# Block products at constant addresses first, then those at register addresses, in the dense passes of a graph network kernel

## What is computed

```python
for l in range(2):
    h = h @ Wt[l].T + bt[l]
    g = tanh(h[row] @ Wg[l] + bg[l])
    norm = g * dinv[row] * dinv[col]
    out = segment_sum(norm[:, None] * h[row], col)
    h = relu(out + h)
```

## Time and profile before

| | |
|---|---|
| time of three runs | 3939.83, 3942.78, 3947.1 us (median 3942.78) |
| the profiled execution | 3943.99 us |
| its span from first to last instruction | 3942.1 us |
| pass 0 (gathers from 607 us) | to 1146 us |
| pass 1 (with the building of items) | 1190 to 1741 us |
| block pass 4 | 3018 to 3456 us |
| block pass 5 | 3487 to 3926 us |

### The profile page before, as it was taken

The page is one execution under the profiler, slowest core; times in us unless marked ns, Lnnn a source line. Parts: engine busy times, 40 slices in busy tenths (PEclk is TensorE's granted clock), DMA queues, the critical chain, the costliest instruction groups (busy, mean ns, idle before and its releaser), DMA issues.

```text
span 3942.1 us, 59800 instructions
## 1 busy us (share of the span) xinstructions
PE 2308.3 (59%) x15144; PEld 2029.6 (51%) x15171; DVE 2210.6 (56%) x5804; ACT 1280.8 (32%) x3481; POOL 2021.6 (51%) x2076
## 2 busy tenths in 40 slices
PE   5972223666655666756756545554556666676665
PEld 4971213555534555545656544454445555665565
DVE  8988916777763555553665565778775222132212
ACT  4210011333220333335777754777762000000000
POOL 2777777777747777735777744777750000000000
PEclk9985555666666665556565667778778999989999
DMA  2210001122131344433333324444441222212221
GB/s 81 68 40 4 4 20 58 53 53 52 53 50 52 117 126 124 130 73 89 81 81 81 80 31 123 129 131 131 131 83 59 75 74 80 74 54 75 79 74 53
DMA packets 151496, 298.20 MB, mean 76 GB/s; under 512 B 49862, under 2 KB 67579, under 8 KB 151091
## 3 DMA queue, kind: packets, MB, share of 16 engines
q0 software_dynamic: 72704, 138.94, 15.1%
q1 hardware_dynamic: 74214, 145.16, 11.7%
q10 hardware_dynamic: 4430, 12.43, 1.0%
HBM read 249.70 MB, written 46.67 MB: 75 GB/s over the span
## 4 chain that ended last, share of the span: by engine, by line
POOL 40%; PE 24%; issue 18%; DVE 11%; ACT 3%; DMA 2%; DVEq 1%; POOLq 0%; ACTq 0%; SPq 0%
POOL arena L710 18%; PE psum L1495 15%; POOL pool L710 13%; POOL rec_dram L687 7%; DVE pool L2118 4%; PE psum L1420 3%; PE psum L1225 2%; ACT pool L882 2%; POOL ACC L710 2%; DVE ACC L2338 1%; PE psum L1263 1%; PE psum L1449 1%; ACT pool L811 1%; PE psum L1100 1%; DVE pool L1717 1%
## 5 line engine op out<-in xcount | busy, mean ns | idle before, releaser
L710 POOL DMA_INDIRECT arena<-tab_dram,tblk x832 | 794.0, 954 | 409.1 <-issue 249.5
L1495 PE MATMUL psum<-arena,pool 128*128 x4096 | 568.7, 293 | 301.3 <-DVE pool L2118 293.8
L1495 PEld LDWEIGHTS psum<-arena,pool 128*128 128x128 f32 x4096 | 527.4, 189 | 343.3 <-issue 342.7
L2118 DVE CAST pool<-pool 128x1024 f32<-128x1024 bf16 x256 | 177.1, 694 | 673.4 <-PE psum L1495 672.8
L687 POOL DMA_INDIRECT rec_dram<-arena,ACC x400 | 395.2, 988 | 196.4 <-issue 119.2
L710 POOL DMA_INDIRECT pool<-tab_dram,arena x416 | 401.1, 964 | 131.4 <-issue 126.4
L1543 PE MATMUL psum<-pool 128*128 128x136 f32 (+1 forms) x1664 | 362.0, 399 | 80.2 <-DVE pool L2262 73.9
L1543 PEld LDWEIGHTS psum<-pool 128*128 128x128 f32 x1664 | 335.3, 290 | 92.4 <-issue 51.7
L1379 PE MATMUL psum<-pool 128*128 128x128 f32 x832 | 192.8, 425 | 294.0 <-DMA pool<-tab_dram,arena 200.4
L710 POOL DMA_INDIRECT pool<-tab_dram,tblk x272 | 277.8, 1021 | 126.3 <-issue 78.6
L1379 PEld LDWEIGHTS psum<-pool 128*128 128x128 f32 x832 | 179.8, 328 | 298.4 <-DVE pool L2131 132.3
(11 more groups left out here) (378 smaller groups left out, 4760.6 us busy)
## 6 DMA issues: line engine op xcount, KB each, us to landing
pool<-items_dram SPq DMA_DIRECT2D x128, 512.0 KB, 3.3
items_dram<-pool SPq DMA_DIRECT2D x128, 256.0 KB, 2.5
pool<-dst_dram SPq DMA_DIRECT2D x104, 256.0 KB, 3.5
arena<-tab_dram,tblk POOLq DMA_INDIRECT x832
HN<-in_edge_attr_dram ACTq DMA_DIRECT2D x23, 500.0 KB
pool<-tab_dram,arena POOLq DMA_INDIRECT x416
rec_dram<-arena,ACC POOLq DMA_INDIRECT x400, 2.1
pool<-tab_dram,tblk POOLq DMA_INDIRECT x272
```

The source lines that it names most:

```text
L710: nc.gpsimd.indirect_dma_start(to[:, j, :], None, tab_dram[k], bass.IndirectOffsetOnAxis(ap=idx[:, G * g + j:G * g + j + 1], axis=0)).then ...
L1495: last = nc.tensor.matmul(psum[:, bass.ds(vals[BITE + j] * P, P)], item, of, start=False, stop=False)
L2118: v.tensor_copy(bite32[slot % 4], bite16[slot]).then_inc(s_cast, 1)
```

## The change

The items are numbered in another way. FIRSTS = 640 items have fixed places: item 25 d + s is, for destination block d and source block s, the **first** tile of d that has edges of s (625 of them and 15 empty ones). The other TILES = 416 items are, one for each tile, **later** items: the source block that begins before the tile's start and still goes on in it. (The edges of a destination block are sorted by source block, so a tile needs at most one later item.) ITEMS is 1056, in 132 packs of 8.

In a block pass the 80 packs of first items come first. Their matmuls have constant addresses and no registers are loaded for them (of packs 78 and 79 only one product each is made, so there are 626). Then come 52 packs of later items, whose 16 block numbers are loaded into registers as before, now from a constant address of `where`. The whole pass is written out; the loop is gone. Items are stored as uint8 instead of bf16, so that a pack has 128 KB. SP loads one pack in a DMA into eight buffers, and DVE casts into six `bite32` buffers instead of four.

The setup has fewer steps on DVE (24 linked small instructions, two rounds of seven over 416 elements, two at the end, against 30, 14 over 512 elements, and six), and one PE round trip less. SP writes six small lists instead of four. In pass 1 DVE makes the ends of the later items (two instructions over 832 elements); ACT and PE make those of the 640 first items only. Packs are built from group 8 on instead of 9, 132 instead of 128, so the last group of pass 1 has three packs instead of two.

```diff
+FIRSTS = 640
+PACK = 8
+ITEMS = FIRSTS + TILES
+PACKS = ITEMS // PACK
-FIRST_PACK = 9
+FIRST_PACK = 8
+HELD = 6
-def bites(eng):
-
-    for u in range(LONG):
-        yield u, u, 0
-    with eng.Fori(1, BITES // LONG, 1) as i:
-        for u in range(LONG):
-            yield LONG * i + u, u, i
+def bites(k):
+
+    firsts = FIRSTS // PACK
+    order = []
+    for q in range(GROUPS):
+        order += list(range(firsts * q // GROUPS, firsts * (q + 1) // GROUPS)) + [firsts + q]
+    order.sort(key=lambda b: b >= firsts)
+    return enumerate(order, PACKS * (k - 4))
...
-        items_dram = nc.dram_tensor("items_dram", (P, ITEMS * P), BF16).ap()
+        items_dram = nc.dram_tensor("items_dram", (P, ITEMS * P), U8).ap()
...
             for k in (4, 5):
-                for n in range(0, BITES, 2):
-                    if k == 5 or n >= LONG:
-                        sp.wait_ge(s_cast, BITES * (k - 4) + n + 2 - LONG)
-                    at = n % LONG * BITE * P // 2
-                    sp.dma_start(pool2[:, at:at + BITE * P].bitcast(BF16), items_dram[:, BITE * P * n:BITE * P * (n + 2)]).then_inc(s_bite[n // 2 % 4], 16)
+                for m, b in bites(k):
+                    if m >= LONG:
+                        sp.wait_ge(s_cast, m + 1 - LONG)
+                    sp.dma_start(bite8[m % LONG], items_dram[:, PACK * P * b:PACK * P * (b + 1)]).then_inc(s_bite[m // 2 % 4], 16)
...
             def block_pass(k):
 
                 table = big[:, 2 * NP:2 * NP + NB * AW]
+                firsts = FIRSTS // PACK
                 clear_sums(k)
                 pe.wait_ge(s_itemrow, ROWS_THERE + 48)
                 pe.wait_ge(s_table, CHUNKS * k)
-                for n, slot, i in bites(pe):
-                    vals = item_regs(n)
-                    pe.wait_ge(s_cast, BITES * (k - 4) + n + 1)
-                    for j in range(BITE):
-                        item = bite32[slot % 4][:, P * j:P * (j + 1)]
-                        of = table[:, bass.ds(vals[j] * AW, D)]
-                        last = nc.tensor.matmul(psum[:, bass.ds(vals[BITE + j] * P, P)], item, of,
-                                                start=False, stop=False)
+                for m, b in bites(k):
+                    vals = item_regs(b - firsts) if b >= firsts else None
+                    pe.wait_ge(s_cast, m + 1)
+                    for j in range(PACK):
+                        item, w = bite32[m % HELD][:, P * j:P * (j + 1)], PACK * b + j
+                        if vals:
+                            last = nc.tensor.matmul(psum[:, bass.ds(vals[G + j] * P, P)], item, table[:, bass.ds(vals[j] * AW, D)],
+                                                    start=False, stop=False)
+                        elif j == 0 or w < NB * NB:
+                            d, of = min(w, NB * NB - 1) // NB, min(w, NB * NB - 1) % NB
+                            last = nc.tensor.matmul(psum[:, d * P:(d + 1) * P], item, table[:, of * AW:of * AW + D], start=False, stop=False)
                     last.then_inc(s_part, 1)
                 close_sums().then_inc(s_part, 1)
...
-                for n, slot, i in bites(dve):
-                    dve.wait_ge(s_bite[slot // 2], bite_loads(k, i))
-                    if k == 5 or there(n - 4):
-                        dve.wait_ge(s_part, parts + n - 3 if there(n - 4) else parts + n - 4)
-                    v.tensor_copy(bite32[slot % 4], bite16[slot]).then_inc(s_cast, 1)
-                dve.wait_ge(s_part, parts + BITES + 1)
+                for m, _ in bites(k):
+                    dve.wait_ge(s_bite[m // 2 % 4], bite_loads(m))
+                    if m >= HELD:
+                        dve.wait_ge(s_part, parts + m - PACKS * (k - 4) - HELD + (1 if m - PACKS * (k - 4) >= HELD else 0))
+                    v.tensor_copy(bite32[m % HELD], bite8[m % LONG]).then_inc(s_cast, 1)
+                dve.wait_ge(s_part, parts + PACKS + 1)
```

More of the change, by code:

```diff
@@ L8 @@
 U32 = mybir.dt.uint32
+U8 = mybir.dt.uint8
 ALU = mybir.AluOpType
@@ L364, in gnn_kernel @@
-        bite16 = [pool2[:, BITE * P // 2 * b:BITE * P // 2 * (b + 1)].bitcast(BF16) for b in range(LONG)]
-        bite32 = [pool2[:, BITE * P * b:BITE * P * (b + 1)] for b in range(4, 8)]
-        where = MT[0:1, 0:2 * ITEMS].bitcast(I32)
+        packed = [FT[:, PACK * P // 4 * b:PACK * P // 4 * (b + 1)].bitcast(U8) for b in range(PACKS_A_GROUP)]
+        bite8 = [pool2[:, PACK * P // 4 * b:PACK * P // 4 * (b + 1)].bitcast(U8) for b in range(LONG)]
+        bite32 = [pool2[:, 2048 + PACK * P * b:2048 + PACK * P * (b + 1)] for b in range(HELD)]
@@ L367, in gnn_kernel @@
+        where = MT[0:1, 0:2 * TILES].bitcast(I32)
         newblk = sb("newblk", [P, 2, SLOTS * H + 1])
@@ L1291, in _ @@
             edge_products(COLS // G - 1, 1)
-            pe.wait_ge(s_itemrow, 1)
-            nc.tensor.matmul(bank[7][:, 510:511], key_before, running[:, NB - 1:NB], start=True, stop=True).then_inc(s_pre, 1)
             pe.wait_ge(s_itemv, 1)
-            for h in range(2):
+            for a, to in enumerate((bank[5][:, 0:TILES], bank[7][0:1, 0:TILES])):
                 for i in range(7):
-                    last = nc.tensor.matmul(bank[5 + 2 * h][0:3, 0:ITEMS // 2], weigh3[:, i, :], reached[:, i, ITEMS // 2 * h:ITEMS // 2 * (h + 1)],
-                                            start=(i == 0), stop=(i == 6))
+                    weights = weigh2[:, i, 0:1].to_broadcast([P, P]) if a == 0 else weigh2[:, i, 1:2]
+                    last = nc.tensor.matmul(to, weights, within_tile[:, i, :], start=(i == 0), stop=(i == 6))
                 last.then_inc(s_itemp, 1)
@@ L1474, in turn_sums, with item_regs @@
                 last.then_inc(s_itemp, 1)
-            def item_regs(n):
+            def item_regs(q):
                 _, vals = nc.values_load_multi_w_load_instructions(
-                    where[0:1, bass.ds(2 * BITE * n, 2 * BITE)], engines=[pe.engine], min_val=0, max_val=NB - 1,
+                    where[0:1, 2 * G * q:2 * G * (q + 1)], engines=[pe.engine], min_val=0, max_val=NB - 1,
                     skip_runtime_bounds_check_because="the table holds block numbers of at most NB - 1")
@@ new lines, in _ @@
+            link(v.scalar_tensor_tensor(first_behind, iota[0:NB, 0:NB], -float(P), none_[0:NB, :], ALU.mult, ALU.subtract))
+            link(v.memset(pad_tile, -1.0))
+            link(v.memset(pad_behind, -FAR))
+            for a in range(2):
+                link(v.scalar_tensor_tensor(bucket4[:, a, 0:NB], none_, FAR, span[:, a, :], ALU.mult, ALU.add))
+            link(v.tensor_scalar(bucket4[:, 2, :], iota[:, 0:28], -float(P), FAR, ALU.mult, ALU.add))
+            link(v.tensor_copy(bucket4[:, 3, :], iota[:, 0:28]))
@@ L2092, in long_pass @@
                             item_tiles()
-                        elif 4 <= g < 4 + (PAIRS + 7) // 8:
-                            for c in range(2 * g - 8, min(2 * g - 6, (PAIRS + 3) // 4)):
+                        elif 3 <= g < 3 + (PAIRS + 7) // 8:
+                            for c in range(2 * g - 6, min(2 * g - 4, (PAIRS + 3) // 4)):
                                 edge_steps(c)
```

148 lines of the change are left out of this document (67 added, 81 removed).

## The result

The changed kernel took 3696.2 us (median of 3691.37, 3695.86, 3696.54 and 3699.26) against 3943.2 us for the kernel before, measured beside it: a ratio of 0.937, with a 95% interval from 0.936 to 0.939. The forecast was 3688 us. The profiled execution took 3691.37 us, its span is 3689.6 us against 3942.1, so 252.5 us less.

What follows compares the result with a forecast made beforehand. It took PE's sequencer, with its register loads and arithmetic, to bound the block passes. From the profiled 3943.99 us, 257.1 less for the passes and 2 more for pass 1 gave 3688.9, as median 3688 us; range 3664 to 3718.

Steps and rivals of the forecast that it cites:

- The bound: Block passes: PE's sequencer sets the pace, 3.2 us for a written-out bite and 3.4 us on average in the loop.
- First items: First part of each block pass: 626 products at constant addresses, 0.223 us each, 139.6 us a pass.
- cold start: Start of each block pass at half clock: 3.4 us extra in pass 4, 2.4 us in pass 5.
- Later packs: Second part of each block pass: 52 packs at the pace of written-out bites, 3.2 us each, 166.4 us.
- The seam: Where first items end and later ones begin: the first register load hides behind queued products, saving 2.5 us a pass.
- Passes in all: Both block passes: 306.9 us against 434.5 and 305.9 against 435.4, together 257.1 us less.
- Cast, DMAs and setup: Uint8 cast (0.70 us), 128 KB loads and stores, setup and list DMAs: all hidden behind other work, cost 0.
- Pass 1: After pass 1's last gather: two more half packs in the last group lengthen the uncovered tail, +2 us.
- Supply: Block passes, first packs: each waits for its own small DMA, +27 us a pass, 3742 us; chance 0.05.
- Straight-line code: Block passes: reading written-out instructions stops or slows PE, +25 or +21 us a pass, 3738 or 3731 us; chance 0.07.
- Gathers get faster: Pass 1: halved item store bytes speed POOL's gathers, giving back up to 25 us, 3664 us; chance 0.08.
- The clock: Block passes: half clock throughout makes them 448 us each, the kernel 3971 us, slower than before; chance 0.03.

Runs made afterwards that it cites:

- the run above: Changed kernel with each DVE one-hot instruction of pass 1 writing 128 of 1024 elements; 4849.2 us beside 4854.7 for the changed kernel.
- both kernels meant for it: Changed kernel with one register load a pass, 4700.7 us; changed kernel meant to keep 52 loads with later products at constant addresses, 3553.5 us.

## Why the prediction was right, and where it was not

**The bound.** That a block pass was bound by PE's sequencer was right: with register loads and arithmetic gone, a pass falls to the array's pace. The count behind it was wrong. The prediction says that each product costs two FUSED_REGOPS and two ALU_OP, 0.212 us. Its rows show 2048 of each, and two passes hold 2048 products: one of each, 0.106 us. The records alone would thus have explained less than half of the sequencer's pace. The rest is time around the instructions: in the changed kernel a product's FUSED_REGOPS begins 0.245 us after the last one's. Taking away the ALU_OP (32 ns) and 10 ns of the other gave 0.102 us a product. The sum was not hurt, because the later packs were priced by the distance of bites in the timeline and not by these records.

**First items.** Forecast 139.6 us and 3.4 (pass 4) or 2.4 (pass 5) for the cold start; measured 141.7 and 142.0. The pace of 0.1115 us a half product was right (median 0.112), the cold start 2.1 and 2.4. Pass 4 paid less than forecast because it began at a higher clock: granted 0.62 from 3025 to 3026 us, 0.50 to 3028 and full from 3030, where the kernel before had 0.50 from 3021 to 3027.

**Later packs.** Forecast 52 x 3.2 = 166.4; the loads came on average 3.21 us apart (median 3.19). Right.

**The seam.** Forecast 2.5 us of lead; measured 2.0, from the start of the first register load to the first product behind it. I cited the Trainium skill ("TensorE: Matmul & The Clock Gate") for a queue of 64 and worked out 3.6 us from it. The trace has 17 half products, 34 loads and matmuls, still to begin between the start of the load and its first product. The measured lead is little over half of what the depth would give. The reading of rows 4 behind "at least 1.1 us is hidden" was weak: at the start of pass 5 the granted clock was 0.50 until 3494 us and 0.74 until 3496, and 16 half products at half clock (16 x 0.215 = 3.4 us) take longer than the sequencer's 3.2. That those three bites ran without a gap thus showed little of the lead at full clock. That 2.5 came out near 2.0 is in part luck.

**Passes in all.** 306.9 and 305.9 forecast, 307.0 and 307.3 measured: 257.1 us of gain forecast, 255.6 found. The agreement to 0.1 us in pass 4 is luck: its first part was 1.5 us shorter than the sum has it (141.5 against 143.0), its second 1.6 longer (165.5 against 163.9).

**The kernel.** For the profiled execution 3688.9 us was forecast and 3691.4 measured. The median of the four runs is 3696.2, because the profiled one was the fastest of them; the forecast of 3688 took it to lie 1.2 below the profiled time, and it lies 4.8 above.

**Cast, DMAs and setup.** All at nothing, as forecast. The cast took 693 ns (0.70 taken). A load landed in 2.0 us (estimate 2.1), a store in 2.0. The rule of the Trainium skill on small DMAs ("DMA: Bandwidth & Descriptors", Bandwidth) did not bite: at 128 KB each and a DMA share of 0.27 the array never waited, even in the kernels whose passes ran at the array's pace.

**Pass 1.** Forecast +2 us; the stages up to pass 4 took 3.6 more. The two more half packs cost what they were put at: from the first copy behind the last gather to the last one it is 6.3 us in the changed kernel (1737.45 to 1743.74) and 4.2 before (1736.59 to 1740.75), 2.1 more. But that first copy already came 0.9 us later, which the forecast put at nothing: the gathers took 1.018 us on average instead of 1.013, 2.0 us in all over 416 of them, and the last began 2.9 us later (1727.9 against 1725.0). The remaining 0.6 us lie in the stages between pass 1 and pass 4.

**The rivals.** *Supply* falls by the kernel with all constant addresses. *Straight-line code* falls too: the page counts 90 instruction packets where that of before has 56, and PE was idle ahead of L1506 for 0.8 us in all. The forecast had only 0.07 for it. *Gathers get faster* falls: half the bytes left them at 1026 ns against 1021 before (all of pass 1's into the pool tile), and the prediction had named DVE's one-hots, which the run above shows to be the cause, as the argument against. *The clock* falls: it was granted at 0.99 and 1.00 in the two parts, at PE busy 100% and 70%.

**What the prediction did not see.** It took the order of the change as given and asked what it saves. It noted that a load of 1.1 us hides behind queued products at the seam and counted that once. The same effect can be had for all 52 loads, in the order that the list of packs has before its last line sorts it: 72 us a pass. A later pack (3.2 us of sequencer) and one and a half plain ones (0.5 each, as read above) need about 3.2 + 1.5 x 0.5 = 4 us of sequencer and 2.5 x 1.79 = 4.5 of the array, so the array sets the pace.

**Left open.** No run has the 52 loads without the arithmetic, since both kernels meant for it lost more than they were to lose; the load's price of 1.16 us is read from the sequencer's starts and fits the sum. What holds the sequencer at a lead of 17 half products was not tested. Why some chips take longer outside of the block passes was not found.

## What to carry to other kernels

Where instructions with register addresses and plain ones feed the same array, compare sequencer time and array time over each short run of work, not over the whole: here the sequencer's lead was some 2 us, so work that is slow to issue was free when scattered among work that is quick to issue, and cost its full price when collected in one place. Price such work by the distance of its starts, not by the records of the register instructions. And take out multiplications of addresses by storing them multiplied: one instruction less was worth 0.102 us a product here.

## What the runs showed of the hardware

- Without a register instruction of PE's sequencer that is recorded with 32 ns (and with 10 ns less in another), the distance from product to product fell from 0.245 to 0.143 us.
- One or two plain packs, six, and 80 all gave the same lead of 2.0 us, 17 half products.
- 104 register loads of 1.10 us each cost next to nothing (1.5 us of idle time in two passes) when each stood behind one or two plain packs of eight products.
- DVE's one-hot work (bf16, two inputs) lengthened POOL's indirect DMA instructions from 0.946 to 1.043 us on average; twice the store bytes made 1.056 of it.
- The changed kernel's block passes took the same within 0.5% on two chips, while the whole kernel before differed by 29 to 30% (3943 against 5080 to 5118 us).
